# Routing of 29 tiles moved into the end of the attention program, rows in a slot found without the totals, three tiles left

## The reference, cut to what matters

```python
def reference(x, ctx_2048, g_xattn, g_ffn, ...):
    # _L0_xattn_ref: kv = outer products of 8 channels of one head; convolved with a kernel of
    # 1024 taps (FFT), plus kv * D; contracted with q = layernorm(x)
    x = x + jnp.tanh(g_xattn[0]) * _L0_xattn_ref(ctx_2048, ctx_2048, _layernorm(x), ssm_kernel, D, 8)
    x = x + jnp.tanh(g_ffn[0]) * _L0_ffn_ref(_layernorm(x), G, gate_w, up_w, down_w, lora_A, lora_B)

def _L0_ffn_ref(x, G, gate_w, up_w, down_w, lora_A, lora_B):
    scores = jax.nn.softmax(jnp.einsum('bsh,he->bse', x, G), axis=-1)
    value, indices = jax.lax.top_k(scores, 2)
    w = jnp.einsum('bsk,bske->bse', value, jax.nn.one_hot(indices, 8, dtype=value.dtype))
    gated = silu(einsum('bsh,efh->bsef', x, gate_w)) * einsum('bsh,efh->bsef', x, up_w)
    out = jnp.einsum('bsef,bse,ehf->bsh', gated, w, down_w)
    out = out + einsum('bser,bse,ehr->bsh', einsum('bsh,erh->bser', x, lora_A), w, lora_B)
```

## Time and profile before

| | us |
|---|---|
| median of 3 runs | 1500.05 |
| the profiled execution | 1499.49 |
| its span, first to last instruction | 1497.7 |
| attention block, up to the barrier | 996.9 |
| from the barrier to `token` | 43.3 |
| from `token` to the first transposes of the slot loop | 8.0 |
| the rest, the slot loop | 449.5 |

### The profile page before, as it was taken

How to read it: one execution, slowest core, us unless ns; L and a number is a source line. 1 busy time by engine, 2 the same in 40 slices (tenths; PEclk the granted TensorE clock), 3 DMA queues, 4 the chain that set the end, 5 groups by cost and what they waited for, 6 DMA issues and landing times. The chain is left out here.

```text
span 1497.7 us, 33735 instructions
## 1 busy us (share of the span) xinstructions
PE 1398.2 (93%) x10290; PEld 1347.3 (90%) x10291; DVE 1152.2 (77%) x1922; ACT 774.7 (52%) x1359; POOL 1117.3 (75%) x985
## 2 busy tenths in 40 slices
PE   3999999999999999999999999933899999999994
PEld 3999999999999999999999999923899999999994
DVE  3999999999999999999999999958354454445452
ACT  5656665666566656665666566410333443343341
POOL 6998999899899989998999899515355555555552
PEclk9999999999999999999999999955999999999997
DMA  6766675777676767676767676436589999999984
GB/s 202 206 217 224 213 229 207 231 207 234 204 228 210 235 201 226 211 228 210 227 210 233 203 226 212 161 130 169 120 199 251 267 232 238 250 271 217 234 179 72
DMA packets 114342, 315.44 MB, mean 211 GB/s; under 512 B 25152, under 2 KB 25664, under 8 KB 114304
## 3 DMA queue, kind: packets, MB, share of 16 engines
q1 hardware_dynamic: 93728, 239.96, 50.9%
q0 software_dynamic: 20576, 75.04, 22.4%
HBM read 215.66 MB, written 100.86 MB: 211 GB/s over the span
## 5 line engine op out<-in xcount | busy, mean ns | idle before, releaser
L536 DVE TENSOR_REDUCE oT<-z 128x128 f32<-128x1280 f32 x256 | 380.5, 1486 | 8.9
L637 PE MATMUL Y<-kvhi,t_hi 128*128 128x288 f32 x1280 | 382.5, 299 | 0.0
L638 PE MATMUL Y<-kvlo,t_hi 128*128 128x288 f32 x1280 | 377.7, 295 | 0.0
L639 PE MATMUL Y<-kvhi,t_lo 128*128 128x288 f32 x1280 | 377.1, 295 | 0.0
L309 POOL TENSOR_TENSOR kvlo<-kv,kvhi 128x1152 fp32r<-128x1152 f32 x128 | 340.7, 2686 | 0.0
L292 POOL TENSOR_TENSOR kv<-cT 128x768 f32<-128x768 f32 x128 | 239.1, 1868 | 9.1 <-DMA cT<-in_c 9.1
L637 PEld LDWEIGHTS Y<-kvhi,t_hi 128*128 128x128 f32 x1280 | 240.5, 188 | 0.6
L638 PEld LDWEIGHTS Y<-kvlo,t_hi 128*128 128x128 f32 x1280 | 240.8, 188 | 0.0
L639 PEld LDWEIGHTS Y<-kvhi,t_lo 128*128 128x128 f32 x1280 | 240.8, 188 | 0.0
L519 DVE TENSOR_TENSOR z<-Y,qT 128x512 f32<-128x512 f32 x256 | 176.8, 691 | 28.2 <-PE Y L639 16.2
L1241 PE MATMUL GU<-wt_hi,xu_hi 128*128 x568 | 170.5, 300 | 0.0
(11 more groups left out here) (174 smaller groups left out, 3266.4 us busy)
## 6 DMA issues: line engine op xcount, KB each, us to landing
cT<-in_c SPq DMA_DIRECT2D x32, 768.0 KB, 8.0
t_hi<-khi SPq DMA_DIRECT2D x64, 384.0 KB, 3.6
t_lo<-klo SPq DMA_DIRECT2D x64, 384.0 KB, 5.0
u_hi<-kshi SPq DMA_DIRECT2D x64, 320.0 KB, 5.8
u_lo<-kslo SPq DMA_DIRECT2D x64, 320.0 KB, 6.8
x_nat<-in_x SPq DMA_DIRECT2D x32, 512.0 KB, 4.1
out<-x_new SPq DMA_DIRECT2D x32, 512.0 KB, 4.8
normed<-n SPq DMA_DIRECT2D x32, 512.0 KB, 7.4
```

What stands on the lines that cost most here:

```text
L536: nc.vector.tensor_reduce(oT[p][:, 2 * r:2 * r + 2, h * IB:(h + 1) * IB], view(z[s][:], [[ZC, 2], [2, IB], [2 * IB, ZS], [1, 2]]), AX.XY, ...
L637: nc.tensor.matmul(out, w_hi[:, w], m_hi[:, c, :], start=start, stop=False)
L638: nc.tensor.matmul(out, w_hi[:, w], m_lo[:, c, :], start=False, stop=False)
L639: return nc.tensor.matmul(out, w_lo[:, w], m_hi[:, c, :], start=False, stop=stop)
```

## The change

- `start_early`, `scale_early`, `choose_early`, `count_early` and `place_early` do the routing for tiles 0 to 28 inside the attention block, VectorE's part in its last two bodies and between the steps of the last two chains. TensorE takes CNT of these tiles (11 matmuls, into `Y[0]`) between `transpose_n2(31)` and `project(31)`. The row in a slot is now the rank modulo 128, which needs no totals, since each expert begins at a whole slot; the slot is the rank divided by 128 plus the expert's first slot, added later.
- The numbered rows (128 wide, the number of the token where the row is the token's) are now made tile by tile, on GpSimd with `tensor_scalar` (`number_rows`) and, for the first choice of tiles 0 to 15, on ScalarE with Square and Relu. GpSimd makes 29 of them at the end of the attention block and 19 behind the barrier.
- `weight` is split in an early store (29 tiles), issued by SyncE at the end of the attention block ahead of the stores of tile 31, and a late one. All 16 `pack` DMAs move to the end of SyncE's list in the attention block. The gate `g_ffn` is loaded with the first constants; `lora_b` is zeroed in the attention block.
- Behind the barrier VectorE routes three tiles (24 elements an instruction), the starts come from one product and one sum (`routed.before`) in place of eight additions, and `is_slot` is made in four pieces that feed TensorE directly, with no product on GpSimd.

```diff
@@ attend, sync, after the last body
+                eng.wait_ge(weighted, 1)
+                eng.dma_start(weight_d[:, early], routed.weight[:, early]).then_inc(routed.weight_out, 16)
                 eng.wait_ge(res_done, NT)
                 eng.dma_start(out_d[NT - 1], x_new[1][:]).then_inc(x_out[1], 16)
                 eng.wait_ge(n2_done, NT)
...
                 eng.wait_ge(w_out, 32 * NT)
+                for e in range(E):
+                    weights.pack(eng, whi_d, bhi_d, e)
+                    weights.pack(eng, wlo_d, blo_d, e)
                 eng.wait_ge(later_in, 16 * len(constants.later))
@@ attend, gpsimd
+                def route_early():
+                    eng.wait_ge(routed.gate_done, 1)
+                    nc.gpsimd.memset(weights.lb[:].bitcast(F32), 0.0).then_inc(weights.lb_zero, 1)
...
+                    eng.wait_ge(sums_done, 1)
+                    nc.gpsimd.tensor_tensor(product[:], routed.scores[:, early], routed.chosen[:, early].bitcast(F32),
+                                            ALU.mult).then_inc(product_done, 1)
+                    eng.wait_ge(routed.cast, 1)
+                    for c, half in FIRST_ROWS:
+                        number_rows(nc.gpsimd, routed, constants, c, half, early)
@@ number_rows, new
+    tiles = [t for t in range(half * NT // 2, (half + 1) * NT // 2) if within.start <= t < within.stop]
+    for t in tiles:
+        ins = engine.tensor_scalar(routed.numbered(c, t), constants.iota[:], routed.row[:, c, t:t + 1],
+                                   constants.number[:, t:t + 1], ALU.is_equal, ALU.mult)
@@ attend, scalar, after the last body
                 high_n2(NT - 1)
+                nc.scalar.activation(dcol[:], epsc[0:NH, :], ACT.Exp)
+                eng.wait_ge(weight_zero, 1)
+                eng.wait_ge(product_done, 1)
+                nc.scalar.mul(routed.weight[:, early, 0:E], product, routed.gate[:, 0:1]).then_inc(weighted, 1)
                 take_small(NT - 1)
@@ attend, vector, after the last body
                 total(NT - 1, 1, 1, 3)
+                scale_early()
                 residual(NT - 1, 1)
+                choose_early(0)
+                invert2(NT - 1)
+                choose_early(1)
+                count_early()
                 take_lr(NT - 2)
-                invert2(NT - 1)
                 low_n2(NT - 1)
+                place_early()
                 take_lr(NT - 1)
@@ attend, tensor, after the last body
                 transpose_n2(NT - 1, 1)
+                eng.wait_ge(z_done, 8 * NT - 1)
+                eng.wait_ge(sums_ready, 2)
+                eng.wait_ge(es, step_at["chosen"])
+                nc.tensor.matmul(CNT, routed.utri[:], routed.chosen[:].rearrange("p t e -> p (t e)"), start=True, stop=False)
...
                 project(NT - 1)
                 turn(NT - 1)
@@ route_tokens, vector
-        for e in range(E):
-            link(V.tensor_tensor(cum[:, e + 1:e + 2], cum[:, e:e + 1], nt[:, e:e + 1], ALU.add))
...
+        link(V.tensor_tensor(sums[:], routed.before[:], nt[:].rearrange("p (o e) -> p o e", o=1).to_broadcast([P, E, E]), ALU.mult))
+        link(V.tensor_reduce(begin[:], sums[:], AX.X, ALU.add))
+        V.tensor_tensor(end[:], begin[:], nt[:], ALU.add).then_inc(begin_done, 1)
...
+        split_places(nc, eng, routed, late, 3)
+        link(V.tensor_tensor(opening[:], one_hot[:].rearrange("p c t e -> p (c t) e"),
+                             begin[:].rearrange("p (o e) -> p o e", o=1).to_broadcast([P, 2 * NT, E]), ALU.mult))
+        link(V.tensor_reduce(slot[:].rearrange("p c t -> p (c t)"), opening[:], AX.X, ALU.add))
+        eng.wait_ge(routed.blocks, 2)
+        link(V.tensor_tensor(slot[:], slot[:], routed.block[:], ALU.add))
+        for c, half in PIECES:
+            part = slice(half * NT // 2, (half + 1) * NT // 2)
+            V.tensor_tensor(is_slot[:, c, part], ..., ALU.is_equal).then_inc(slots_done[c][half], 1)
@@ route_tokens, gpsimd
+        number_rows(nc.gpsimd, routed, constants, 1, 1, early)
+        eng.wait_ge(routed.cast, 2)
+        number_rows(nc.gpsimd, routed, constants, 0, 1, late)
+        number_rows(nc.gpsimd, routed, constants, 1, 1, late)
@@ route_tokens, tensor
+        for c, half in PIECES:
+            eng.wait_ge(routed.rows_done[c][half], waits[c, half])
+            eng.wait_ge(slots_done[c][half], 1)
+            for t in range(half * NT // 2, min((half + 1) * NT // 2, TE)):
+                nc.tensor.matmul(IDX[:, 0:SG], routed.numbered(c, t), is_slot[:, c, t, :], start=first, stop=False)
```

More of the change, by code:

```diff
@@ L146, in attend @@
         shared_y = view(OP[:], [[HALF, 2], [1, YC]])
+        early, late = routed.early, routed.late
+        free = qT[0][:].rearrange("p h c w -> p (h c w)")
+        left, mark, product = [free[:, n * TE * E:(n + 1) * TE * E].rearrange("p (t e) -> p t e", e=E) for n in range(3)]
+        ranked = free[:, 3 * TE * E:5 * TE * E].rearrange("p (c t e) -> p c t e", c=2, e=E)
+        best = routed.place[:, 0, early]
+        CNT = Y[0][:, 0, 0:NT * E]
         later_in = sem("later_in")
@@ new lines, in place_early, with body @@
+                def place_early():
+                    eng.wait_ge(early_counted, 1)
+                    link(V.tensor_tensor(ranked, routed.one_hot[:, :, early],
+                                         CNT[:, 0:TE * E].rearrange("p (o t e) -> p o t e", o=1, e=E).to_broadcast([P, 2, TE, E]), ALU.mult))
+                    link(V.tensor_reduce(routed.place[:, :, early], ranked, AX.X, ALU.add))
+                    split_places(nc, eng, routed, early, 0)
+                def body(i, p, k, first=False, last=False, starts=False):
@@ L609, in body @@
                     total(i, p, 1, 0)
+                    if starts:
+                        start_early()
                     if not first:
@@ L761, in _ @@
+                for s in range(1, NT // GT):
+                    mm = nc.tensor.matmul(grouped[:, s:NT // GT], routed.ones[:],
+                                          groups[:, 0:NT // GT - s, :].rearrange("p g (o e) -> p g o e", o=1)
+                                          .to_broadcast([P, NT // GT - s, GT, E]), start=False, stop=s == NT // GT - 1)
+                mm.then_inc(early_counted, 1)
                 project(NT - 1)
                 turn(NT - 1)
[L765 to L778, removed]
@@ L781 @@
[L781 to L811, removed]
-            for part, d in ((self.hi, whi_d), (self.lo, wlo_d)):
-                eng.dma_start(part[:, e % 2, cols].bitcast(F32), d[NT // E * e + q, :, 0:WQ]).then_inc(self.landed, 16)
-            if singly:
-                eng.wait_ge(self.landed, LANDED * e + 32 * (q + 1))
@@ L1056, in route_tensor @@
+        for c in range(2):
+            eng.wait_ge(routed.rows_done[c][1], 2)
+            for t in range(TE, NT):
+                mm = nc.tensor.matmul(IDX[:, 0:SG], routed.numbered(c, t), is_slot[:, c, t, :], start=False,
+                                      stop=c == 1 and t == NT - 1)
         mm.then_inc(idx_done, 1)
```

394 lines of the change are left out of this document (252 added, 142 removed).

## The result

The changed kernel takes 1513.51 us, the median of 4 runs (1511.93 to 1514.31), against 1500.09 for the kernel before on the same chip: 1.0084 times as long, interval 1.0072 to 1.0096. It is slower by 13.4 us, outside the range of the prediction (1495.5 to 1508.5). Its profiled execution took 1514.31 us, the slowest of the four, with a span of 1512.5 us; the profiled execution before had 1497.7, so the two traces differ by 14.8.

A forecast was written before the change was run, and what follows sets the result against it. Time was taken as set by the barrier's opening and `token` behind it: the barrier takes 17.0 us, the routing gives 15.4, so +1.6 on the median 1500.05, say 1501.8 us; range 1495.5 to 1508.5.

The forecast's parts named there:

- The two marks: Barrier opening at 1013.9, 17.0 us later, and `token` 27.9 us behind it instead of 43.3: `token` shifts by +1.6 us.
- rival (c): TensorE's clock rises in IDX, now one unbroken stretch, saving some 4 us: 1497.5; chance 0.1.
- the clash: Behind the barrier, VectorE's ten short two-input instructions each wait half a GpSimd instruction: +2.2 us, bounds 0 and 5.
- the price of a GpSimd row: Ahead of the barrier, 29 `tensor_scalar` at 0.45 us end at 1010.8, inside SyncE's time; GpSimd decides from 0.54 on.
- rival (a): GpSimd holds the barrier: at 0.75 us per `tensor_scalar` it opens 6 us later, clash worth 1.5 more, 1509; chance 0.17.
- The tail: Attention block's end: early steps under cover cost nothing, `transpose_n2(31)` +2.05 us, compute engines at the barrier near 999.3, not 996.9.
- b: Time in us after the barrier opens; IDX was put at 13.5, `token` at 27.9, bounds 25.5 and 31.5.
- SyncE's list: Early weight store, tile 31's stores, then 16 packs at 0.68 us bring SyncE to the barrier at 1013.4, deciding its opening.
- `token` to XU: From `token` to the first transposes, 7.96 us of gathers and tables that the change leaves as they are.
- The slot loop: The loop behind the routing is the same program, with no change in time forecast.
- The start: One more small DMA ahead of `ag` and one more Tanh delay the start: +0.4 us, bounds 0 and 0.7.

The follow-up runs named there:

- e6: Changed kernel with SyncE's packs early and 24 added GpSimd `tensor_scalar` of 128x128, eight each of three forms, in idle time; 1513.30 us.
- e4: Changed kernel with `start_early` in body 31 instead of 30 and its Exp behind ScalarE's last body; 1507.67 us.
- e5: Changed kernel with the four `opened` DMAs issued ahead of GpSimd's 19 rows behind the barrier; 1512.73 us.
- e9: e8 with GpSimd's 4 rows of the attention block moved behind the barrier, 16 rows there; 1488.13 us, 0.9916 times the kernel before.
- e1: Changed kernel with SyncE's 16 packs right behind the last split-weight store of tile 31 and the early weight store last; 1512.99 us.
- e2: Changed kernel with all 29 GpSimd rows of the attention block moved behind the barrier, SyncE's list as it is; 1525.06 us.
- e3: Changed kernel with both edits: the 29 GpSimd rows behind the barrier and SyncE's packs early; 1506.82 us.
- e8: e7 with `g_ffn` loaded with the later constants and its Tanh at the attention block's end; 1487.28 us, 0.9921 times the kernel before.
- after: The changed kernel itself, without further edits; 1513.51 us, 1.0084 times the kernel before.
- e7: Changed kernel with e1's list, e4's start, `opened` issued in the attention block, GpSimd's 48 rows shared with VectorE and ScalarE; 1488.67 us, 0.9929 times the kernel before.
- e10: e9 with 18 added matmuls of 128x512, result unused, between IDX and the first XU; 1488.14 us, 0.9913 times the kernel before.

## Why the prediction was wrong

**The view of the kernel was right as far as it went.** The two marks, the barrier and `token`, moved the time by +25.7 and -17.9 us, and behind the barrier the change does what was forecast. Another 7.05 us arose behind `token`, where the forecast had nothing. IDX took 13.9 us from its first matmul to `token` (forecast 14.4), at clock 0.50, so rival (c) is refuted. `is_slot` started 9.97 us behind the barrier, against 9.85 without the clash.

**The step that failed is the price of a GpSimd row**, "With 0.45 it is through at 1010.8, inside SyncE's time". The form cost 0.78, so the 29 took 22.6 us in place of 13.1: +9.5 us. I had written the threshold myself ("It decides from 0.54 us on"), which makes this rival (a), given 0.17. Its own price, 1509, was 4.5 us short of the result, by the terms below. The bounds, 0.2 and 0.47, were both rows of other forms (a memset and a product), and I took them as bounds because they were the nearest, though I wrote that two per-row scalars could raise the price. Two-input work was no upper bound: e6 shows one `tensor_scalar` with a single operation dearer (0.60) than the product (0.47). The sentence on the Trainium skill ("GPSIMD Engine Reference", section 4.1) pointed the same wrong way; here one-input work runs on GpSimd at a third of VectorE's speed (0.79 against 0.26 us), and the measurement decides.

**The tail came 2 us later than forecast, for the most part by a stall priced at nothing.** "VectorE has 1.9 us idle in 30, so nothing": the subtraction of `start_early` reads two SBUF tiles and met GpSimd's 1152-element product (937.05 to 942.43). It took 2.20 us instead of 0.40, `take_lr(30)` came at 993.00 instead of 991.05, and GpSimd's rows began at 999.69 instead of 997.7. Of these 2 us the later start of the whole run is 0.4 (first convolution matmul at 25.21, before 24.80), for which the forecast had a term of its own. e4 takes the neighbour away and with it the stall. The rule that I applied only behind the barrier (the Trainium skill, "SBUF — State Buffer", "Who interferes with whom": such a pair blocks each other) applied here too; the case agrees, 0.40 against 2.20. Rows and start give 997.7 + 2.0 + 22.6 = 1022.3, the barrier.

**The clash behind the barrier was sized too large**, 2.2 us with a blocked half instruction each. Five of VectorE's short two-input instructions lost 0.11 to 0.16 us each (0.29 to 0.34 beside 0.18), some 0.7 us, and e5 shows the 0.18 without the rows. Others with two inputs, such as L1086, took 0.18 beside the rows too, and in e5 a few with one input were slow as well (0.49 for `row_i`, 0.22 in the changed kernel), so the price isn't one per two-input instruction. GpSimd's rows lost next to nothing beside this chain, 0.80 against 0.78. What they lost came from the long instructions: beside the four back-to-back pieces of `is_slot` one row took 3.94 us and the next 2.12, some 4.5 us together. That pair of long and short was in no forecast. Here it only delayed the `opened` DMAs, in e9 it cost 1.81 us of IDX. IDX began at b = 11.5, where 13.5 was forecast, and took 13.9 us to `token` instead of 14.4, so `token` came at b = 25.35, 2.5 under the forecast.

**SyncE's list** was sized well: 2.48 us for the issue behind the weight store, a wait of 3.4, packs at 0.68, and the end at 1016.06 instead of 1013.4, of which 2 us are the late tail. It holds second: e1 shows that it cost nothing here, e2 against e3 that it would cost some 17 us alone. Since both held, taking either away gives little or nothing, and the whole gain comes when both go.

**`token` to XU was not costed.** "Gathers and tables that the change leaves as they are" is true of the instructions and false of their place: four `opened` DMAs on GpSimd's queue were moved behind 19 rows, to 1042.43, and their landing, not `token`, released the gather. +1.75 us, and e5 returns it.

**The slot loop** was taken as the same program and hence the same time: +5.3 us, of them 2.9 at the lower clock and 1.8 evenly in all slots, cause not found. **The start**, +0.4, is neither confirmed nor refuted (e8).

In sum: 1.6 forecast, +8.7 at the barrier, -2.5 in the routing, +1.75 to XU, +5.3 in the loop, 14.8 in all.

## What to carry to other kernels

Work moved ahead of a barrier is only free while the list of every engine ends before the work that held the barrier until then (here the last logits). Price each list by that engine's own row of the same form. A form that was never measured needs a bound above the nearest row and not at it, above all where the margin that decides (here 0.45 against 0.54) is small. Cost moved DMAs by what is queued ahead of them. Look for a GpSimd neighbour at each two-input VectorE instruction that is put anywhere, also where the engine seems to have room, and read the longest of a group and not only its mean. Where two lists hold one barrier, undo both before judging the idea: the version with rows shared out by price is at 1487.3 us, 0.79% faster than the kernel before.

## What the runs showed of the hardware

- GpSimd `tensor_scalar`, 128x128 float32: 0.60 us with one operation, 0.64 with two and constants, 0.79 with two and two operands per row (e6, after). VectorE takes 0.26 for the dearest of these, ScalarE 0.30 a pass (e7).
- Beside short VectorE instructions such a row stays at 0.80 us (after, e7). Beside four back-to-back VectorE instructions of 1152 elements with two SBUF inputs (5.26 us in all), one row took 3.94 us and the next 2.12; e1, e3, e4 and e5 show the same two, 3.94 to 4.16 and 2.12.
- The issue that follows a store of 3712 pieces takes 2.48 us where 0.34 to 0.44 is usual (e1's list has `out` at 0.34 when it isn't behind that store). The pieces are those of 29 tiles by 128 rows.
- In the first slots the clock stayed at 1.00 in the six traces where it rose by 8.5 us behind the first XU, and fell back to 0.50 for some 3 us in the five where it rose at 9.2 us or later. In e10 TensorE was granted 1.00 at the first XU and 0.50 within the 2.45 us of idle time behind it. The beginning of the loop comes out at 22.4 to 22.9 or at 24.3 to 25.3 us, with nothing between in twelve traces.
